# Cross-attention and mixture of experts on one core: scores computed transposed, DMA transposes replaced by block transposes and block moves

## The chip, the cores and the metric

The kernel runs on one core of a Trainium2 chip. The metric is device time in microseconds from start to end of one execution. TensorE (PE) multiplies matrices into PSUM, VectorE (DVE), ScalarE (ACT) and GpSimd (POOL) work on tiles of 128 partitions, and SyncE (SP) issues most DMAs.

## What is computed

One layer on x (4096 tokens, width 512) with a context of 3202 rows: cross-attention with a single head of width 512, then a top-2 router over 16 experts with a gated feed-forward of width 256 and a capacity of 512 rows per expert.

```python
x = x + attn(k=ctx, v=ctx, q=layernorm(x))        # softmax(q Wq^T (ctx Wk^T)^T / sqrt(512)) (ctx Wv^T + bv) Wo^T + bo
g = softmax(layernorm(x) @ w_router)              # 16 experts, the two highest are taken
h = silu(rows_e @ w_gate[e]) * (rows_e @ w_fc[e]) # rows_e: at most 512 rows of expert e
x = x + sum over the two experts of g * (h @ w_proj[e])
```

## The kernel before

Every f32 operand of a large product is split in two f16 parts, high and low, and `three_passes` (L41 to L47) multiplies high by high, high by low and low by high, so one product is three matmuls, on L45, L46 and L47. The program has three blocks that follow one another.

`setup` folds the weights (Wq with Wk into `m_w`, Wv with Wo into `g_w`), then turns the 25 full context tiles with a DMA transpose each (`transpose_c`, L194) into `cT`, and computes keys `kT` (512 wide, transposed) and values `vv` in eight PSUM banks. The context has 25 x 128 + 2 rows; the last two are "the tail". Their values are computed at the end of the block and written three times into `v_tail` by DMA (L299). The first query is prepared here as well.

`attend` goes through 32 tiles of 128 queries. TensorE's `step(t)` computes the scores of tile t + 1 (`scores`, 7 chunks: 6 of 512 keys and one of 130; the queries are the stationary operand and the keys stream) and then the values of tile t (`times_values`, 25 key tiles x 3 matmuls of 512 columns, then one matmul for the tail, L1036). VectorE copies each chunk out of PSUM and takes its maximum on the way (`evacuate`, L818), so that the maximum of a query is a number per partition. ScalarE takes the exponential of the whole row with that number as its bias and adds it up on the way (L760), then makes the high part (L765), and VectorE the low part (L840). Two DMA transposes of 25 blocks each (`transpose_p`, L653) turn these into `pT`, keys on partitions, as the product with the values needs them. Queries (`transpose_q`, L618) and router rows (`store_rows`, L635) are turned by DMA transposes too; only the last rows are turned by TensorE (`rows_T`). After the values `residual` on VectorE adds the residual and takes the statistics, GpSimd the power for the deviation, and `route` and `place` choose experts and positions. GpSimd scatters the choice to a table in DRAM. The order of work on each engine is the order in which the code is written; engines meet in semaphores alone.

`experts` gathers each expert's rows from DRAM, turns them on TensorE (L1502), multiplies (`up`, `down`), scales on ScalarE (`out_rows`) and scatters with addition on GpSimd (L1248); at the end the sums are loaded, corrected and stored.

## Time and profile before

| | us |
|---|---|
| median of 3 runs | 1644.28 |
| lowest, highest | 1640.95, 1647.89 |
| the profiled execution, its own time | 1646.86 |
| its span | 1645.0 |
| PE busy in the span | 1542.0 (94%) |
| DVE, ACT, POOL busy | 822.8, 444.7, 342.7 |

Times in the rows are microseconds from the span's start unless marked ns. A matmul's record lasts longer than its share of the engine, since matmuls are pipelined: what one costs in a stream is the distance between two starts. "Idle before" in brackets is time in which the engine had no work, and behind the arrow stands what released it.

### The profile page before, as it was taken

The page shows a single profiled execution, that of the slowest core. Times are in us where ns is not written, and L with a number is a line of the kernel's source. Part 1 is how long each engine was busy: PE and PEld are TensorE (multiplying, and loading weights), DVE is VectorE, ACT ScalarE, POOL GpSimd, SP SyncE. Part 2 cuts the span into 40 slices and gives each one's busy share as a digit, 9 for nine tenths or more (in the row PEclk, how much of TensorE's full clock was granted, in tenths as well). Part 3 has the DMA queues.
Part 4 walks back from the last instruction along what each step waited for, and adds up shares of the span by engine and source line. Part 5 has one row for each costly group of instructions (what it writes and reads, how often), then busy time and mean ns, then how long its engine had stood idle before and what let it go on. Part 6 is the DMA issues. An engine that isn't in the chain of part 4 may idle for free. (4 is left out here: it accounts for less than half of the span.)

```text
span 1645.0 us, 23544 instructions
## 1 busy us (share of the span) xinstructions
PE 1542.0 (94%) x7953; PEld 723.1 (44%) x7953; DVE 822.8 (50%) x2323; ACT 444.7 (27%) x537; POOL 342.7 (21%) x449
## 2 busy tenths in 40 slices
PE   7999889999999999999999999999996499999953
PEld 3444434444444444444444444444442245555520
DVE  4433245555555555554555555555554555555524
ACT  2332131231123212221222122311230244545430
POOL 1000001111111121112111211111111455665530
PEclk9999999999999999999999999999998699999975
DMA  7542135543554345434543454335432479899769
GB/s 211 119 102 49 52 73 118 105 91 78 110 112 91 78 103 120 91 78 96 120 97 78 88 121 96 86 80 118 102 83 62 141 187 232 200 205 223 153 105 370
DMA packets 372863, 198.52 MB, mean 121 GB/s; under 512 B 309528, under 2 KB 325918, under 8 KB 372832
## 3 DMA queue, kind: packets, MB, share of 16 engines
q1 hardware_dynamic: 350368, 154.04, 39.7%
q0 software_dynamic: 16896, 35.42, 11.4%
q10 hardware_dynamic: 5568, 8.67, 1.4%
q8 instruction: 17, 0.28, 0.1%
q14 instruction: 14, 0.11, 0.0%
HBM read 78.78 MB, written 43.81 MB: 75 GB/s over the span
## 5 line engine op out<-in xcount | busy, mean ns | idle before, releaser
L45 PE MATMUL sc<-kT,qt 128*128 128x512 f16 (+1 forms) x896 | 316.8, 359 | 9.4 <-PEq L184 4.9
L46 PE MATMUL sc<-kT,qt 128*128 128x512 f16 (+1 forms) x896 | 316.4, 358 | 0.0
L47 PE MATMUL sc<-kT,qt 128*128 128x512 f16 (+1 forms) x896 | 314.6, 358 | 0.0
L47 PE MATMUL acc<-vv,pT 128*128 128x512 f16 x775 | 293.6, 379 | 0.0
L46 PE MATMUL acc<-vv,pT 128*128 128x512 f16 x775 | 293.6, 379 | 0.0
L45 PE MATMUL acc<-vv,pT 128*128 128x512 f16 x775 | 293.5, 379 | 0.0
L818 DVE TENSOR_SCALAR_CACHE_REDUCE s_sb<-sc 128x512 f32<-128x512 f32 (+1 forms) x224 | 141.3, 631 | 194.6 <-PE sc L47 194.6
L771 ACT ACTIVATE row<-xs 128x512 f16<-128x512 f32 x32 | 20.2, 630 | 566.9 <-DVE xs L869 566.9
L840 DVE TENSOR_TENSOR p_hl<-p_sb,p_hl 128x3200 f16<-128x3200 f32 (+2 forms) x33 | 111.8, 3391 | 59.1 <-ACT p_hl L765 59.1
L45 PEld LDWEIGHTS sc<-kT,qt 128*128 128x128 f16 x896 | 88.0, 98 | 109.1 <-issue 19.1
L47 PEld LDWEIGHTS sc<-kT,qt 128*128 128x128 f16 x896 | 88.1, 98 | 92.0 <-issue 2.4
L46 PEld LDWEIGHTS sc<-kT,qt 128*128 128x128 f16 x896 | 88.1, 98 | 88.4 <-issue 2.0
L1248 POOL DMA_INDIRECT y_dram<-o_sb,sidx x64 | 102.4, 1601 | 103.0 <-ACT o_sb L1291 86.4
L760 ACT ACTIVATE p_sb<-s_sb,negb 128x3202 f32<-128x3202 f32 x32 | 95.0, 2970 | 87.7 <-DVE negb L826 87.7
L47 PEld LDWEIGHTS acc<-vv,pT 128*128 128x128 f16 x775 | 75.7, 98 | 91.6
L718 POOL TENSOR_TENSOR idf<-ia,ic 128x2 f32<-128x2 f32 x32 | 6.3, 197 | 520.8 <-DVE ia L926 520.8
L46 PEld LDWEIGHTS acc<-vv,pT 128*128 128x128 f16 x775 | 75.7, 98 | 80.7
L45 PEld LDWEIGHTS acc<-vv,pT 128*128 128x128 f16 x775 | 75.6, 98 | 80.8
L765 ACT ACTIVATE p_hl<-p_sb 128x3200 f16<-128x3200 f32 (+2 forms) x33 | 91.9, 2789 | 2.9
L858 DVE SCALAR_TENSOR_TENSOR x<-acc,rinv,xb 128x512 f32<-128x512 f32 x32 | 24.0, 751 | 130.4 <-PE acc L1036 130.4
L731 POOL TENSOR_TENSOR rstd_q<-var_q,nhalf 128x1 f32<-128x1 f32 x31 | 17.1, 550 | 281.3 <-DVE var_q L936 281.3
L1238 POOL DMA_INDIRECT rows<-rows_dram,gidx x64 | 67.8, 1059 | 34.1 <-issue 18.9
(247 smaller groups left out, 2154.5 us busy)
## 6 DMA issues: line engine op xcount, KB each, us to landing
xq<-in_x_dram SPq DMA_DIRECT2D x32, 256.0 KB, 2.8
x_in<-in_x_dram SPq DMA_DIRECT2D x32, 256.0 KB, 3.0
raw_g<-in_L_ffn_w_gate_dram SPq DMA_DIRECT2D x16, 512.0 KB
raw_f<-in_L_ffn_w_fc_dram SPq DMA_DIRECT2D x16, 512.0 KB
raw_p<-in_L_ffn_w_proj_dram SPq DMA_DIRECT2D x16, 512.0 KB
y_dram<-x SPq DMA_DIRECT2D x32, 256.0 KB, 3.0
rows_dram<-row SPq DMA_DIRECT2D x32, 256.0 KB, 2.2
y_sb<-y_dram SPq DMA_DIRECT2D x16, 512.0 KB, 17.4
```

Of the source, the lines that this page charges most:

```text
L45: pe.matmul(out, s_hi, m_hi, start=first, stop=False)
L46: pe.matmul(out, s_hi, m_lo, start=False, stop=False)
L47: return pe.matmul(out, s_lo, m_hi, start=False, stop=last)
L731: pool.tensor_tensor(rstd_q[:], var_q[:], nhalf[:], ALU.pow).then_inc(q_rstd, 1)
L760: act.activation(p_sb[:], s_sb[:], ACT.Exp, bias=negb[:], scale=SM / (XN_S * CTX_S), accum_out=rsum[:]).then_inc(exp_done, 1)
L765: act.activation(p_hl[:, 0, a * P:b * P], p_sb[:, a * P:b * P], ACT.Copy).then_inc(p_hi, 1)
L771: act.activation(row16[:, 0:D], xs2[:], ACT.Copy, scale=XN_S).then_inc(xs_hi, 1)
L818: dve.tensor_scalar(s_sb[:, 512 * c:512 * c + width[c]], sc[c % 3][:, 0:width[c]], 1.0, None, ALU.mult, ALU.max, accum_out=mxc[:, c:c + 1] ...
L840: dve.tensor_tensor(p_hl[:, 1, a * P:b * P], p_sb[:, a * P:b * P], p_hl[:, 0, a * P:b * P], ALU.subtract).then_inc(p_lo, 1)
L858: dve.scalar_tensor_tensor(out=x1[:], in0=acc[:], scalar=rinv[:], in1=xb[:], op0=ALU.mult, op1=ALU.add).then_inc(x1_rdy, 1)
L1238: pool.indirect_dma_start(rows[:, e % 2, 2 * D * j:2 * D * (j + 1)], None, rows_dram, bass.IndirectOffsetOnAxis(ap=gidx[:, e, j:j + 1], ax ...
L1248: pool.indirect_dma_start(y_dram, bass.IndirectOffsetOnAxis(ap=sidx[:, e, j:j + 1], axis=0), o_sb[:, e % 2, j, :], None, bounds_check=Y_LA ...
```

## The change

In `setup` the context tiles and the first two queries are turned by TensorE (`turns`) in two extra PSUM buffers and copied out by ScalarE and VectorE in turn; keys and values go through six banks in one sequence (`items`). The tail's values are computed as full tiles with the tail row repeated (`cT_wide`), so that no DMA is needed. In `attend` the keys are the stationary operand and the queries stream, so the scores come out transposed, keys on partitions, 128 columns per matmul. The maximum of a query then lies across partitions: it is folded on VectorE, turned by TensorE (`greatest`), reduced, made a diagonal and spread to all partitions by a matmul with ones (`spread`), and subtracted before the exponential. The sum is taken by GpSimd (`sums`) and a matmul with ones (`row_sum`). The scores buffer `s_T` exists twice. The tail has its own small scores and is added on VectorE in `residual`. Queries and router rows are turned in 32 x 32 blocks by VectorE, stored in DRAM, and loaded back block by block. In `experts` the end is in another order and its last products use four banks. The core of the diff:

```diff
 # setup, TensorE
+                def turns(kind, n):
+                    i = job[kind, n]
...
+                    for q in range(2 * KT):
+                        last = pe.transpose(turn[i % 2][:, q * P:(q + 1) * P], rows[:, q * P:(q + 1) * P], ident16[:])
+                    last.then_inc(t_pe, 1)
+                for i in range(TAIL):
...
+                    for t in range(KT):
+                        last = three_passes(pe, vt_bank[i][:],
+                                            (cT_wide[:, t * TAIL + i, :], cT_wide[:, (KT + t) * TAIL + i, :]),
+                                            (g_w[:, t, 0, :], g_w[:, t, 1, :]), t == 0, t == KT - 1)
+                        keys(n, k)
+                        if G4 * (n + 1) + k < NK:
+                            turns("c", G4 * (n + 1) + k)
 # attend, SyncE
+                def blocks_in(dest, blocks, done):
+                    for i in range(NB):
+                        sp.dma_start(dest[BL * i:BL * (i + 1)].rearrange("d k (g c) -> d k g c", c=BL),
+                                     blocks.rearrange("(g d) (k i c) -> i d k g c", d=BL, i=NB, c=BL)[i]).then_inc(done, 16)
-                    for h in range(2):
-                        sp.dma_start_transpose(pT[:, h], p_hl[:, h]).then_inc(pT_in, 16)
+                    if post:
+                        store_x1(t - 1)
+                        store_rows(t - 1)
+                        store_row_blocks(t - 1)
+                    if more_q:
+                        load_xq(t + 3)
+                    if post:
+                        load_row_blocks(t - 1)
+                    if turn_q:
+                        turn_query(t + 2)
 # attend, ScalarE
+                def copied(t, h, c):
+                    a, b = chunk[c]
+                    act.wait_ge(sc_pe, NCH * t + c + 1)
+                    if not isinstance(t, int) or t > 1:
+                        act.wait_ge(p_lo, NG * (t - 2) + group_of(a) + 1)
+                        act.wait_ge(sum_rdy, t - 1)
+                    act.activation(s_T[h][:, a:b, :].rearrange("p k c -> p (k c)"), sc[c % 3][:, 0:(b - a) * P],
+                                   ACT.Copy).then_inc(sc_cp, 1)
+                    if not isinstance(t, int) or t > 0:
+                        act.wait_ge(pv_part, NG * (t - 1) + g + 1)
+                    act.activation(pT[:, 0, a:b, :], s_T[h][:, a:b, :], ACT.Copy).then_inc(p_hi, 1)
 # attend, VectorE
+                        dve.tensor_tensor(rm[:, 0:b - a, :], so_far, s_T[h][:, a:b, :], ALU.max)
...
+                    dve.wait_ge(mx_pe, t + 1)
+                    dve.reduce_max(mx[:], ps_x[:, 0:P + TAIL], AX_X)
+                    dve.drain()
+                    dve.tensor_scalar(diag[:], ident[:], mx[:], None, ALU.mult).then_inc(dg_rdy, 1)
...
+                    dve.wait_ge(mb_pe, t + 1)
+                    dve.tensor_copy(m_b[:], ps_y[:, 0:P]).then_inc(mb_rdy, 1)
+                    dve.drain()
+                    for g, (a, b) in enumerate(groups):
+                        dve.tensor_tensor(s_T[h][:, a:b, :], s_T[h][:, a:b, :], m_b[:].unsqueeze(1).to_broadcast([P, b - a, P]),
+                                          ALU.subtract).then_inc(sub_rdy, 1)
+                    dve.transpose(row_bl[:], row16[:]).then_inc(rb_rdy, 1)
+                    dve.transpose(q_bl[:], q16[:]).then_inc(qb_rdy, 1)
 # attend, TensorE
+                    for n in range(a, b):
+                        for k in range(KT):
+                            keys_high, keys_low = (kT[:, h * KT + k, n * P:(n + 1) * P] for h in range(2))
+                            last = three_passes(pe, sc[c % 3][:, (n - a) * P:(n - a + 1) * P], (keys_high, keys_low),
+                                                (q_t[:, k, :], q_t[:, KT + k, :]), k == 0, k == KT - 1)
+                def greatest(t):
+                    pe.wait_ge(rm_rdy, t + 1)
+                    pe.transpose(ps_x[:, 0:P], rm1[:], ident[:]).then_inc(mx_pe, 1)
+                def spread(t):
+                    pe.wait_ge(dg_rdy, t + 1)
+                    wait_for(pe, rinv_rdy, t)
+                    pe.matmul(ps_y[:, 0:P], ones_f[:], diag[:], start=True, stop=True).then_inc(mb_pe, 1)
+                def row_sum(t):
+                    pe.wait_ge(sum_rdy, t + 1)
+                    pe.wait_ge(mb_rdy, t + 1)
+                    pe.matmul(ps_y[:, P:P + 1], sum1[:], ones_f[:, 0:1], start=True, stop=True).then_inc(rs_pe, 1)
+                        if k == 0:
+                            row_sum(t)
+                        if more and k == 3:
+                            greatest(t + 1)
+                        if more and k == 6:
+                            spread(t + 1)
+                        if post and k == (12 if more else 18):
                             logits(t - 1)
 # experts, TensorE
-                step(E // 2 - 1, 1, True, False)
                 for j in range(J):
-                    down(E - 1, j, 1)
+                    down(E - 2, j, 0)
+                for u in range(4):
+                    up(E // 2 - 1, 1, u)
+                last_down(E - 1, 1)
```

How this moves instructions is seen best on three queues. PE in the loop's body where scores end and values begin, now: the scores are followed by the tail's scores into ps_x, then values with the three f32 pieces in between.

```order
L47 MATMUL sc<-qt,kT 128x128
L45 MATMUL ps_x<-kT,qt 128x2
...
L47 MATMUL acc<-vv,pT 128x512
L1245 MATMUL ps_y<-ones_f,sum 128x1
...
L1234 MATMUL ps_x<-ident,rm 128x128
...
L1240 MATMUL ps_y<-diag,ones_f 128x128
```

Before, L47 of the last chunk (128x130) was followed by values at once, and one matmul (L1036) came at their end. The sum now stands after the first key tile, the transpose of the maxima after the fourth, the spread after the seventh.

VectorE in the loop's body from the fifth full chunk of scores to the fold of the maxima, now (rm is the running maximum, s_T the scores, rs_v and rinv belong to the tile before):

```order
L998 TENSOR_TENSOR rm<-rm,s_T 128x512
L1139 SCALAR_TENSOR_TENSOR q<-xqs,q 128x512
L996 REGISTER_ALU
L998 TENSOR_TENSOR rm<-rm,s_T 128x128
L1028 TENSOR_TENSOR rs_v<-p_tail 128x1
L1029 COPY p_held<-p_tail 128x2
L1032 TENSOR_TENSOR rs_v<-ps_y,rs_v 128x1
L1034 TENSOR_SCALAR rs_v<-rs_v 128x1
L1036 RECIPROCAL rinv<-rs_v 128x1
L1003 TENSOR_TENSOR rm<-rm 128x256
L1005 TENSOR_TENSOR rm<-rm 128x128
```

Before, the same place read:

```order
L818 TENSOR_SCALAR s_sb,mxc<-sc 128x512
L944 SCALAR_TENSOR_TENSOR q<-xqs,q 128x512
L815 REGISTER_ALU
L818 TENSOR_SCALAR s_sb,mxc<-sc 128x130
L824 TENSOR_REDUCE mx<-mxc 128x1
L826 TENSOR_SCALAR negb<-mx 128x1
```

The inverse of the sum has moved from the step's start to this place, and it waits there for TensorE's `row_sum`.

SyncE's loop body now:

```order
L735 DMA x_in<-in_x_dram 128x512
L739 ISA
L739 DMA y_dram<-x 128x512
L743 ISA
L743 DMA rows_dram<-row 128x1024
L753 DMA blocks_r<-row_bl 128x1024
L732 ISA
L732 DMA xq<-in_x_dram 128x512
L756 REGISTER_ALU
L748 DMA xrT<-blocks_r 32x32x32 x4
L762 DMA blocks_q<-q_bl 128x1024
```

and behind these four loads of qt from blocks_q (L748). Before, the body began with the two transposes of p_hl (L653) and had one transpose each for row and q.

## Rows read from the trace of the kernel before

**Rows 1.** Stretch: length; busy (count) PE, PEld, DVE, ACT, POOL; PEclk, DMA, GB/s.

```profile
228.90:1224.00 995.10, 995.10 (x5118) 461.43 (x5115) 523.90 (x1772) 228.88 (x236) 147.33 (x263) 1.00 0.45 97
```

**Rows 2.** Timeline of PE, one step: start us, us, engine line op, operands.

```profile
610.04 0.38 PE L47 MATMUL acc<-vv,pT 128*128 128x512 f16 x1
610.35 0.39 PE L1036 MATMUL acc<-v_tail,tailT 6*128 6x512 f16 x1
610.67 0.39 PE L45 MATMUL sc<-kT,qt 128*128 128x512 f16 x1
610.89 0.38 PE L46 MATMUL sc<-kT,qt 128*128 128x512 f16 x1
...
643.54 0.39 PE L1036 MATMUL acc<-v_tail,tailT 6*128 6x512 f16 x1
```

**Rows 3.** Timeline of PE in that step: the last chunk of scores, and the router's matmuls.

```profile
626.33 0.22 PE L45 MATMUL sc<-kT,qt 128*128 128x130 f16 x1
...
627.00 0.38 PE L45 MATMUL acc<-vv,pT 128*128 128x512 f16 x1
...
628.95 0.25 PE L1057 MATMUL ps_m<-w_r,xrT 128*128 128x32 f16 x4
...
629.15 0.38 PE L45 MATMUL acc<-vv,pT 128*128 128x512 f16 x1
```

**Rows 4.** Timeline of PE in setup: f32 matmuls of 128 columns.

```profile
43.34 1.05 PE L454 MATMUL bank<-ident,raw_g 128*128 128x128 f32 x8
```

**Rows 5.** Groups by form: line engine op operands xcount | busy us, mean ns | idle before.

```profile
L258 ACT ACTIVATE kT<-bank 128x512 f16<-128x512 f32 x24 | 14.3, 597 | 39.9 <-PE bank L47 39.9
L944 DVE SCALAR_TENSOR_TENSOR q<-xqs,q 128x512 f16<-128x512 f32 x31 | 21.3, 687 | 0.0
L313 DVE SCALAR_TENSOR_TENSOR kT<-bank,kT 128x130 f16<-128x130 f32 x4 | 1.2, 291 | 0.9 <-ACT kT L258 0.9
L1355 DVE COPY xTe<-tp 128x1024 f16<-128x1024 f16 x32 | 22.0, 688 | 13.8 <-PE tp L1502 8.6 <-issue 5.2
L1350 DVE SCALAR_TENSOR_TENSOR wp<-raw_p,wp 128x1024 f16<-128x1024 f32 x16 | 19.4, 1215 | 0.0
L840 DVE TENSOR_TENSOR p_hl<-p_sb,p_hl 128x3200 f16<-128x3200 f32 x31 | 108.3, 3493 | 59.1 <-ACT p_hl L765 59.1
L45 PEld LDWEIGHTS sc<-kT,qt 128*128 128x128 f16 x896 | 88.0, 98 | 109.1 <-issue 19.1
```

**Rows 6.** Timeline of DVE: small operations that wait for one another.

```profile
629.65 0.17 DVE L892 SCALAR_TENSOR_TENSOR lg<-ps_m,lg 128x16 f32<-128x16 f32 x1
629.90 0.17 DVE L878 TENSOR_REDUCE m<-lg 128x1 f32<-128x16 f32 x1
```

**Rows 7.** DMA: ScalarE's queue in 0 to 8 and 0 to 14 us; issues, us to landing.

```profile
q10 hardware_dynamic: 373, 0.26, 13.2%
...
q10 hardware_dynamic: 1204, 0.27, 11.6%
...
rows_dram<-row SPq DMA_DIRECT2D x32, 256.0 KB, 2.2
...
qt<-q SPq DMA_TRANSPOSE x32, 3.5
```

**Rows 8.** Timeline of PE: starts after idle time in setup and first tiles.

```profile
13.73 0.55 PE L432 MATMUL bank<-ident,tail_f 2*128 2x2 f32 x4 [2.07 <-DMA tail_f<-in_ctx_dram]
...
47.81 0.38 PE L45 MATMUL bank<-cT,m_w 128*128 128x512 f16 x1 [3.42 <-DMA cT<-c]
...
186.82 0.58 PE L45 MATMUL sc<-kT,qt 128*128 128x512 f16 x1 [4.85 <-PEq L184]
...
210.02 0.58 PE L45 MATMUL sc<-kT,qt 128*128 128x512 f16 x1 [4.55 <-DMA qt<-q]
```

**Rows 9.** Timeline of PE and POOL: last logits of attention, last expert's scatter.

```profile
1268.97 0.29 PE L1057 MATMUL ps_m<-w_r,xrT 128*128 128x32 f16 x4 [0.52 <-DVE xrT L992]
...
1584.91 1.54 POOL L1248 DMA_INDIRECT y_dram<-o_sb,sidx  x1 [5.41 <-DMA y_dram<-o_sb,sidx]
```

More of the change, by code:

```diff
@@ L300, in _ @@
-                act.wait_ge(s_vt, 48)
+                        item_high(n, "k", k)
+                        if late is not None:
+                            turned("c", late)
+                        late = G4 * (n + 1) + k if G4 * (n + 1) + k < NK else None
+                        if k == 2 and n in x_after:
+                            query_high(x_after[n])
+                    item_high(n, "v", 0)
+                    if late is not None:
+                        turned("c", late)
+                    for j in range(1, G4):
+                        item_high(n, "v", j)
+                        if j == 2 and n in x_after:
+                            turned("x", x_after[n])
@@ L377, in _ @@
                     dve.wait_ge(w_hi, KT + u + 1)
[L378 removed]
+                    dve.scalar_tensor_tensor(out=m_w[:, u, 1, :], in0=m_bank[u][:], scalar=W_S, in1=m_w[:, u, 0, :],
                                              op0=ALU.mult, op1=ALU.subtract).then_inc(w_lo, 1)
+                turned("c", 3)
                 for n in range(NC):
[L382 removed]
+                    late = None
+                    for k in range(G4):
@@ new lines, in _ @@
+                        if late is not None:
+                            turned("c", late)
+                        late = G4 * (n + 1) + k if G4 * (n + 1) + k < NK else None
+                        if n in x_after:
+                            query(x_after[n], k)
+                    item_low(n, "v", 0)
+                    if late is not None:
+                        turned("c", late)
+                    for j in range(1, G4):
+                        item_low(n, "v", j)
+                        if j == 2 and n in x_after:
+                            turned("x", x_after[n])
@@ L489, in attend, with group_of @@
     R12, PP, P12, OH2, tot1 = (v[n] for n in ("R12", "PP", "P12", "OH2", "tot1"))
-    NCH = -(-S // 512)
-    width = [min(512, S - 512 * c) for c in range(NCH)]
-    SKIP = float(1 << 20)
-    NK_A = (NK + 1) // 2
-    parts = ((0, NK_A), (NK_A, NK))
+    CH = 4
+    NCH = -(-NK // CH)
+    chunk = [(CH * c, min(CH * (c + 1), NK)) for c in range(NCH)]
+    groups = ((0, 2 * CH), (2 * CH, 4 * CH), (4 * CH, NK))
+    NG = len(groups)
+    SKIP = float(1 << 20)
+    BL = 32
+    NB = P // BL
+    assert TAIL == 2
+    def group_of(tile):
+        return [a <= tile < b for a, b in groups].index(True)
     with ExitStack() as c_:
@@ L779, in query_high, with step @@
                 def query_high(t):
-                    act.wait_ge(q_xs, t)
-                    act.wait_ge(q_in, 16 * t)
+                    act.wait_ge(q_xs, t - 1)
+                    wait_for(act, qb_rdy, t - 2)
                     act.activation(q16[:, 0:D], xqs[:], ACT.Copy, scale=XN_S).then_inc(q_hi, 1)
-                def step(t, post, more, more_q):
-                    if post:
+                def step(t, h, post, more, more_q, copies=True):
+                    for c in range(NCH if more and copies else 0):
+                        copied(t + 1, 1 - h, c)
+                        if c == 2 and post:
+                            rows_high(t - 1)
+                        if c == 4 and more_q:
+                            query_high(t + 2)
+                    if post and not more:
@@ new lines, in _ @@
+                exponentials(0, 0, 1)
+                copied(1, 1, 4)
+                high(0, 0, 1)
+                exponentials(0, 0, 2)
+                copied(1, 1, 5)
+                high(0, 0, 2)
+                copied(1, 1, 6)
+                query_high(2)
+                step(0, 0, False, True, True, False)
+                step(1, 1, True, True, True)
+                with act.Fori(1, NT // 2 - 1) as m:
+                    for h in range(2):
+                        step(2 * m + h, h, True, True, True)
@@ L1031, in times_values @@
                             logits(t - 1)
[L1032 removed]
+                        if post and k == (23 if more else NK - 1):
                             places(t - 1)
[L1035 to L1047 removed]
```

821 lines of the change are left out of this document (462 added, 359 removed).

## The prediction

> **What bounds the kernel now.** I read the stretches first, then TensorE's order of time inside one step, then the groups of the other engines and the DMA queues, and last the edges where TensorE is idle. From 228.90 to 1224.00 us TensorE is busy for all of 995.10 us at granted clock 1.00, the 2.4 GHz level, while VectorE is busy 524 us, ScalarE 229 and GpSimd 147 [rows 1]. Busy time alone could hide slow matmuls, so I checked the spacing. One step of the loop over query tiles runs from the tail matmul at 610.35 to the next at 643.54, 33.19 us; inside it a 512-column matmul follows the last after 0.215 us, and the tail lies in 0.63 us (610.04 to 610.67) [rows 2]. The twelve 130-column matmuls take 627.00 - 626.33 = 0.67 us, 56 ns each, and the eight of the router 0.20 us (628.95 to 629.15) [rows 3]. So 72 x 0.2155 + 0.67 = 16.19 us for scores, 75 x 0.2155 = 16.16 for values, 0.2 for the router, about 0.06 for places, 0.63 - 0.215 = 0.41 for the tail and 0.1 for its transpose make 33.1. Nothing in the step waits. The DMA transposes and all softmax work are hidden already: **the steady step gains nothing from what is removed**, and everything new on TensorE is paid 30 times.
>
> **The change, part by part.**
>
> *TensorE's step.* Scores become 25 x 4 x 3 = 300 matmuls of 128 columns. At 56 ns per 130 columns [rows 3] that is 55.5 ns each: 16.65, +0.46. The two tail keys become 12 matmuls of 2 columns, each with a full weight load; the router's narrow ones cost 0.20 / 8 = 25 ns, so +0.3. The old tail (0.41 + 0.1) goes. Three f32 pieces come in: the sum over keys, the transpose of the maxima, the spread of the maximum. Eight f32 records of 128 columns took 1.05 us [rows 4], at most 0.13 each; five records, two of them one column wide: +0.5. Together 33.19 + 0.46 + 0.3 - 0.5 + 0.5 = about 33.9, **+0.74 per step** (0.5 to 0.9).
>
> *A new wait on TensorE.* The transpose in `greatest` stands after four key tiles of values (the PE rows of the order), and behind it waits the rest of values, the whole engine. Let T be the start of values. The transpose is reached at T + 12 x 0.2155 + 0.2 = T + 2.8. Before that the fifth full chunk of scores ends at T - 0.84 (0.33 of tail and 0.67 of the last chunk lie behind it, less a drain); ScalarE copies it (0.60), VectorE takes the maximum (512 wide, 0.69), the low part of the query (0.69), the maximum of the last tile (0.29) [rows 5], the five small operations of `inverse`, 0.25 apart [rows 6], and folds of 256 and 128 elements (0.43 by the same rate, 0.29). This adds up to T + 3.3, and the f32 weight load after it is exposed, 0.2: a stall of 0.75 us. VectorE may also be behind at its head: between chunks 2.67 us apart it now does the block transpose of a row (1024 elements f16, between a copy of that size, 0.69, and a two-input operation, 1.22 [rows 5]) and the query's statistics. At 1.22 this makes ScalarE's `query_high` late, and the copy of the fifth chunk stands behind it: another 0.65. I take **1.0 us per step**, between the two (0 if VectorE overlaps more than I allow; 2 if each of the dozen handovers costs 0.1 more). The next new matmul, `spread`, comes 1.9 us later and needs about 1.3: free.
>
> *VectorE, ScalarE, GpSimd.* Per step VectorE does maxima 3.8, folds, diagonal and broadcast copy 1.6, subtraction of the maximum 3.8 and low parts 3.8 (3200 elements at 3.49 us, in three pieces [rows 5]), two block transposes 2.4, residual passes and statistics 3.3, and some 9 of query, rows, routing and places: about 28 of 34 us, against 17.5 now. ScalarE does about 13. GpSimd gets sums of 3456 elements; even at twice VectorE's time each that is 8 us, beside its 5. None becomes the bound by its sum; VectorE matters by its order alone. The first two thirds of the probabilities are ready some 18 us ahead of their use; the last third waits for values to end and is used 16 tiles into the next.
>
> *DMA.* Gone are two transposes of 25 blocks and two of 8. New per step are two stores of 256 KB (2.2 us, as rows_dram [rows 7]) and twice 4 loads of 1024 pieces of 64 bytes. SP waits in its queue for the query's and the row's blocks, with the next tile's loads behind; those have a whole step. For the pieces: in the first 8 us ScalarE's queue moved 373 packets in 13.2% of 16 x 8 us, in the first 14 us 1204 in 11.6% of 16 x 14 [rows 7]; the 831 between, nearly all of 4 bytes, cost (26.0 - 16.9) / 831 = 11 ns. On the other side the DMA transpose of a query, 1024 packets, lands after 3.5 us [rows 7]. So the four loads, 256 packets on each of 16 engines, take between 256 x 11 ns + 2 = 5 us and 4 x 3.5 = 14 us. I take 7, nearer the tiny packets, since these are plain packets too. Queries: blocks leave VectorE at T + 6.5, are in DRAM at 8.8 and turned at about 16; scores want them at T + 18. Rows: turned at about T + 7, wanted at T + 10. Hidden, with 2 to 3 us to spare.
>
> *Setup and the first tiles.* TensorE now turns 25 context tiles and 2 queries: 27 x 8 x 55.5 ns = +12.0. The two tail values are 24 matmuls instead of 12: +2.6. Against this, no wait for context transposes and no cold clock after it (3.42 idle [rows 8]), -5.4; projections no longer behind tail_f (2.07 [rows 8] and the ScalarE copies after), -2.7; no v_tail DMAs in the 4.85 before attention [rows 8], -3.4; second scores not after a DMA (4.55 idle, then cold again [rows 8]), -6. The two scores cost +1.6, more constants +1.5, and the first values wait for the first sums, +3. Together **+3**.
>
> *Last step and tail.* Rows of tile 30 go through DRAM while only values run: turned about 20 us after the step began, logits wanted at 12, and places and routing stand before the last residual: +6. Then the last row's blocks cost 1.2 + 2.3 + 7 instead of the 1.9 us that ended with the logits at 1268.97 [rows 9], plus two residual passes, 1.5: +10. Together **+16**.
>
> *Experts' end.* The last scatter waited 5.41 us for the previous expert's [rows 9], whose outputs now are written a whole `up` earlier: **-5**.
>
> Sum: 30 x 1.74 = 52, + 3 + 16 - 5 = **+66 us**. The profiled execution took 1646.86 us (span 1645.0), 0.2% over the median of 1644.28; I apply the sum to the median: **1710 us**.
>
> **The rivals.**
> 1. *Long narrow streams run slower than twelve do.* For: nothing here shows 300 in a row. Against: the spacing does not grow from the first to the twelfth, 56 ns [rows 3]. A weight load record lasts 98 ns [rows 5]; if loads no longer hid under matmuls half as long, a step would cost 300 x (98 - 55.5) = 12.8 us more, and even half of that is 1710 + 32 x 6.4 = 1915. It shows from 3 ns a matmul on. 4 in 100. The Trainium skill (TensorE: Matmul & The Clock Gate, Back-to-back issue gap) gives about 81 ns for a sustained pair of weight load and 128-column matmul, which by its figure would make a step 7.7 us longer, an estimate of 1955 us; the trace's 56 ns disagrees.
> 2. *The block moves are late.* The query's loads have no slack left at 9 us and decide from there: at 10, 1740; at 14 scores wait 5 us a step and the rows' loads hold logits 4 more, 1710 + 30 x 5 to 30 x 9 = 1860 to 1980. For: no 64-byte packets in the trace, and SP issues eight such loads a step. Against: 4-byte packets at 11 ns. 16 in 100, more than half of it at the small end. The Trainium skill (VectorE: DVE Perf Modes, The three transpose paths) warns that a plain DMA copy that transposes by strides is 19 times slower than a DMA transpose where the innermost destination stride is large. By its factor one query would take 66 us and the kernel over 3000; no run shows it, and the 64-byte runs here are whole.
> 3. *Not slower: the edges pay for the steps.* Its place is VectorE's chain between the last scores and `greatest`. If that ends before T + 2.8, and a 128-column matmul costs only its columns at 2.4 GHz, 53.3 ns, a step is 33.19 - 0.2 + 0.3 - 0.5 + 0.5 = 33.3; then 30 x 0.1 = +3, and with the first stretch at -4, the end of attention at +6 and the experts at -7 the sum is -2: 1642. It decides where the step stays under 33.4. Against: 56 ns is measured, and tail scores and f32 pieces are real work. 7 in 100, of which 3 pass to faster.
> 4. *The new wait never shows*, the rest as forecast: 1680. This is the low end of my case, not beside it.
>
> **The numbers.** My case, a step of 33.7 to 36 us: 73 in 100, 1710. Its bounds are +20 (30 x 0.5, and edges +5) and +109 (30 x 2.8, and edges +25), 1664 to 1753; the small end of rival 2 takes the top to 1775. Range **1664 to 1775**; it leaves out rival 1, rival 3 and the rest of rival 2, 18 in 100. A measurement of this kernel tells 0.5%, 8 us, from no change. Faster by more 0.03, within 0.04, slower 0.93.
>
> **What would show it.** In the profile after: a step of 34.3 to 35.5 us; narrow matmuls 55 to 56 ns apart; before `greatest` an idle TensorE of about 1 us, released by VectorE's fold; none before scores from the loads of qt, none before logits from those of xrT until the last step, which has 6 to 9; first values at about 228. It is wrong if the step is under 33.5 or over 36, or if the query's loads release the scores.

## The result, and the profile after

The changed kernel takes **1823.08 us** (median of 4 runs, 1821.14 to 1826.18) against 1644.54 for the kernel before on the same chip (1640.95 to 1647.89): ratio **1.109**, interval 1.106 to 1.112. Slower was forecast, but by 66 us; it is 178.5, and 1823 lies above the range. The profiled execution took 1826.18 us, its span 1824.5, that is 179.5 more than the span before. I cut both spans at the same four events, from TensorE's timelines:

| Stretch | before, us | after, us | more | forecast |
|---|---|---|---|---|
| start to the first values | 229.0 | 236.5 | +7.5 | +3 |
| 30 steps, first values to values of tile 30 | 995.5 (33.18 each) | 1156.3 (38.54 each) | +160.8 | +52 |
| from there to the experts' first table matmul | 61.3 | 77.3 | +16.0 | +16 |
| experts | 359.3 | 354.4 | -4.9 | -5 |

The start, the end of attention and the experts differ from the forecast by 4.6 us together, nearly all of it at the start; a step costs 5.36 us more where 1.74 was written. The stretches after, first the 30 steps, then a stretch of 38.74 us that ends at the transpose in `greatest`, about one step, and two pieces behind that transpose (length; busy time and count of PE, PEld, DVE, ACT, POOL; PEclk, DMA share, GB/s):

```profile
236.51:1392.79 1156.28, 1062.34 (x12051) 765.79 (x12052) 928.00 (x1864) 365.74 (x566) 514.39 (x503) 0.97 0.27 54
664.20:702.94 38.74, 34.34 (x403) 25.14 (x403) 32.08 (x66) 12.27 (x19) 17.26 (x17) 1.00 0.29 57
702.94:704.18 1.24, 1.24 (x6) 0.64 (x7) 0.80 (x4) 0.06 (x1) 0.00 (x0) 1.00 0.50 47
704.18:708.00 3.82, 3.82 (x12) 1.80 (x11) 2.47 (x3) 0.24 (x1) 0.00 (x0) 0.55 0.18 69
```

TensorE, busy all the time before [rows 1], is idle 94 us of these steps. VectorE went from 17.5 us a step to 928.00 / 30 = 30.9, and 32.1 in the stretch of 38.74. The last row is TensorE near the 1.2 GHz level. TensorE's timeline around `greatest` and the list of its waits show where both come from:

```profile
702.94 0.33 PE L1234 MATMUL ps_x<-ident,rm 128*128 128x128 f32 x1 [3.41 <-DVE rm L1005]
703.10 0.38 PE L45 MATMUL acc<-vv,pT 128*128 128x512 f16 x1
...
704.98 0.63 PE L46 MATMUL acc<-vv,pT 128*128 128x512 f16 x1
705.40 0.63 PE L47 MATMUL acc<-vv,pT 128*128 128x512 f16 x1
```
```profile
PE ps_x L1234 <- DVE rm L1005: 93.9, 30, 3.5
PE ps_m L1274 <- DMA xrT<-blocks_r: 17.7, 1, 17.7
```

The wait is the one forecast, at its place and with its releaser, VectorE's fold; but it lasts 93.9 / 30 = 3.1 us, not 1.0. From 704.2 on its matmuls are 0.43 us apart instead of 0.215. This does not happen in every step: slow matmuls stand behind 19 of the 30 transposes, 7 to 12 at a time, and cost 31 us in all, 1.0 us a step on average. From the fourth step on a step without them lasts 37.8 us (37.76 from the transpose at 665.18 to the one at 702.94), a step with them 38.8 to 40.1. The second row is the last tile's router rows; it is the only wait for blocks.

Everything else on TensorE is as it was written. The narrow matmuls and the twelve of the tail, from its timeline ahead of the values that start at 696.64:

```profile
696.28 0.22 PE L47 MATMUL sc<-qt,kT 128*128 128x128 f16 x1
696.33 0.17 PE L45 MATMUL ps_x<-kT,qt 128*128 128x2 f16 x1
...
696.61 0.16 PE L47 MATMUL ps_x<-kT,qt 128*128 128x2 f16 x1
696.64 0.38 PE L45 MATMUL acc<-vv,pT 128*128 128x512 f16 x1
```

So why is VectorE late? Its own timeline around that transpose, and GpSimd's at the same moments. The small operations are those of [rows 6]; `hit` marks the highest logit, `oh` is the chosen expert as a row of ones and zeros:

```profile
689.87 1.68 DVE L998 TENSOR_TENSOR rm<-rm,s_T 128x512 f32<-128x512 f32 x1 [0.54 <-ACT s_T L898]
...
711.79 0.17 DVE L1073 TENSOR_REDUCE m<-lg 128x1 f32<-128x16 f32 x1
712.04 1.30 DVE L1075 SCALAR_TENSOR_TENSOR hit<-lg,m,rev 128x16 f32<-128x16 f32 x1
713.41 0.17 DVE L1078 TENSOR_REDUCE r<-hit 128x1 f32<-128x16 f32 x1
713.66 1.08 DVE L1080 TENSOR_SCALAR oh<-rev,r 128x16 bf16<-128x16 f32 x1
```
```profile
689.74 1.25 POOL L827 TENSOR_TENSOR xb<-x_in,bo_row 128x512 f32<-128x512 f32 x1
...
712.04 2.67 POOL L858 TENSOR_TENSOR sum<-sum,s_T 128x512 f32<-128x512 f32 x2 [0.39 <-issue]
714.92 4.22 POOL L858 TENSOR_TENSOR sum<-sum,s_T 128x512 f32<-128x512 f32 x3 [0.20 <-issue]
```

An operation on 16 numbers takes 1.30 us, a reduction of the same 16 numbers 0.17, and the slow ones coincide with GpSimd's additions. Over the whole run, the groups by form, of after, then of before:

```profile
L998 DVE TENSOR_TENSOR rm<-rm,s_T 128x512 f32<-128x512 f32 x128 | 120.4, 941 | 68.3 <-ACT s_T L898 57.9 <-issue 9.5
L1080 DVE TENSOR_SCALAR oh<-rev,r 128x16 bf16<-128x16 f32 x64 | 68.5, 1071 | 5.0
L1075 DVE SCALAR_TENSOR_TENSOR hit<-lg,m,rev 128x16 f32<-128x16 f32 x64 | 45.3, 708 | 5.4
L1093 DVE SCALAR_TENSOR_TENSOR lg<-oh,lg 128x16 f32<-128x16 bf16 x32 | 35.1, 1098 | 2.4
```
```profile
L880 DVE SCALAR_TENSOR_TENSOR hit<-lg,m,rev 128x16 f32<-128x16 f32 x64 | 15.0, 235 | 5.4
L885 DVE TENSOR_SCALAR oh<-rev,r 128x16 bf16<-128x16 f32 x64 | 15.0, 234 | 5.3 <-issue 0.5
L898 DVE SCALAR_TENSOR_TENSOR lg<-oh,lg 128x16 f32<-128x16 bf16 x32 | 5.6, 175 | 2.4
```

That gave **theory A**: VectorE's queue sets the step, because GpSimd's new additions (L858, 860, 863) hold its operations up. **Rival B**: VectorE's total is beside the path; the badly placed wait at `greatest` and the slow clock behind it are the cost themselves.

### The profile page after: what moved, and what is told of

Read it like the earlier page. It is cut to its first block and busy times, and to the rows that moved or that the text cites. A ratio compares the mean times of both kernels' runs of the same rounds, so it can differ in the third digit from the quotient of the medians.

```text
span 1824.5 us, 40730 instructions
## 1 busy us (share of the span) xinstructions
PE 1620.5 (89%) x15565; PEld 1057.9 (58%) x15565; DVE 1253.2 (69%) x2427; ACT 602.0 (33%) x902; POOL 735.4 (40%) x708
## 5 line engine op out<-in xcount | busy, mean ns | idle before, releaser
L45 PE MATMUL sc<-qt,kT 128*128 128x128 f16 x3100 | 520.8, 219 | 3.4 <-POOL before L821 3.4
L46 PE MATMUL sc<-qt,kT 128*128 128x128 f16 x3100 | 520.9, 219 | 0.0
L47 PE MATMUL sc<-qt,kT 128*128 128x128 f16 x3100 | 520.8, 219 | 0.0
L47 PE MATMUL acc<-vv,pT 128*128 128x512 f16 x800 | 316.0, 395 | 0.0
L45 PEld LDWEIGHTS sc<-qt,kT 128*128 128x128 f16 x3100 | 303.3, 98 | 8.8 <-POOL before L821 3.9
L46 PEld LDWEIGHTS sc<-qt,kT 128*128 128x128 f16 x3100 | 303.3, 98 | 2.2
L47 PEld LDWEIGHTS sc<-qt,kT 128*128 128x128 f16 x3100 | 303.3, 98 | 0.0
L858 POOL TENSOR_TENSOR sum<-s_T 128x512 f32<-128x512 f32 x32 | 72.8, 2274 | 400.5 <-ACT s_T L909 400.5
L858 POOL TENSOR_TENSOR sum<-sum,s_T 128x512 f32<-128x512 f32 (+1 forms) x160 | 208.7, 1305 | 31.9 <-issue 17.4
L898 ACT ACTIVATE s_T<-sc 128x512 f32<-128x512 f32 (+1 forms) x224 | 118.2, 545 | 231.9 <-PE sc L47 216.9
L998 DVE TENSOR_TENSOR rm<-rm,s_T 128x512 f32<-128x512 f32 (+1 forms) x160 | 129.8, 811 | 73.2 <-ACT s_T L898 57.9
L909 ACT ACTIVATE s_T<-s_T,e_bias 128x1024 f32<-128x1024 f32 (+1 forms) x96 | 112.8, 1179 | 110.2 <-DVE s_T L1018 110.2
L47 PEld LDWEIGHTS acc<-vv,pT 128*128 128x128 f16 x800 | 80.7, 101 | 103.3 <-issue 15.3
L1024 DVE TENSOR_TENSOR pT<-s_T,pT 128x1024 f16<-128x1024 f32 (+1 forms) x96 | 127.7, 1354 | 6.1 <-ACT pT L918 6.1
L1018 DVE TENSOR_TENSOR s_T<-s_T,m_b 128x1024 f32<-128x1024 f32 (+1 forms) x96 | 116.2, 1266 | 2.9
L918 ACT ACTIVATE pT<-s_T 128x1024 f16<-128x1024 f32 (+1 forms) x96 | 104.3, 1087 | 27.5 <-PE acc L47 26.6
L1234 PE MATMUL ps_x<-ident,rm 128*128 128x128 f32 x32 | 11.9, 370 | 93.9 <-DVE rm L1005 93.9
```

What stands on the lines that cost most here:

```text
L45: pe.matmul(out, s_hi, m_hi, start=first, stop=False)
L46: pe.matmul(out, s_hi, m_lo, start=False, stop=False)
L47: return pe.matmul(out, s_lo, m_hi, start=False, stop=last)
L858: pool.tensor_tensor(sum4[:, 0:b - a, :], before_it, s_T[h][:, a:b, :], ALU.add)
L898: act.activation(s_T[h][:, a:b, :].rearrange("p k c -> p (k c)"), sc[c % 3][:, 0:(b - a) * P], ACT.Copy).then_inc(sc_cp, 1)
L909: act.activation(s_T[h][:, a:b, :], s_T[h][:, a:b, :], ACT.Exp, bias=e_bias[:], scale=SM / (XN_S * CTX_S)).then_inc(ex_rdy, 1)
```

## The experiments

Each ran against the kernel before on its own chip. Four chips were used, and the kernel before took 1644.1 to 1646.7 us on them, so runs of different groups can be compared to 2 or 3 us. "Step" is the start of values of tile 30 less that of tile 0, through 30; it comes from the profiled execution, the time is the median of all, and executions of one kernel differ by some 3 us, 0.1 us a step.

### e1_no_sums: GpSimd adds next to nothing

```diff
-                    for c in range(1, NCH):
...
-                        pool.tensor_tensor(sum4[:, 0:b - a, :], before_it, s_T[h][:, a:b, :], ALU.add)
...
+                    pool.wait_ge(ex_rdy, NG * t + NG)
                     wait_for(pool, rs_pe, t)
-                    pool.tensor_tensor(sum1[:], sum4[:, 0, :], sum4[:, 1, :], ALU.add).then_inc(sum_rdy, 1)
+                    pool.tensor_tensor(sum1[:], s_T[h][:, 0, :], s_T[h][:, 1, :], ALU.add).then_inc(sum_rdy, 1)
```

> Leaves out most of the sum over keys (one addition of two key tiles is left), so the row sum is not the real one; all else is as in the change. Theory A (VectorE's queue sets the step of 38.5 us, because GpSimd's additions hold up VectorE's small operations of route): the two operations on hit fall from 1.30 and 0.83 us to about 0.23 each, the two on oh from 1.08 to 0.24, the second on lg to 0.17, together 3.5 to 4.5 us less of VectorE's step; the wait before greatest falls from 3.1 us to under 1, step 34.3 to 35.5, time 1700 to 1735. Rival B (the wait at greatest comes from the order of the chain between the last scores and the transpose alone, what GpSimd does is beside the path): the wait stays at 3 us, step 38.4, time within 10 of 1823.

1723.37 us, ratio 1.048 (1.045 to 1.050); step 35.35. Its groups and its wait at `greatest`:

```profile
L991 DVE TENSOR_TENSOR rm<-rm,s_T 128x512 f32<-128x512 f32 x128 | 88.7, 693 | 103.7 <-ACT s_T L891 95.9 <-issue 7.0
L1068 DVE SCALAR_TENSOR_TENSOR hit<-lg,m,rev 128x16 f32<-128x16 f32 x64 | 16.0, 250 | 5.4
L1073 DVE TENSOR_SCALAR oh<-rev,r 128x16 bf16<-128x16 f32 x64 | 15.0, 234 | 4.9
```
```profile
PE ps_x L1227 <- DVE rm L998: 33.9, 30, 2.9
```

The operations are short again, and 100 us are gone. The wait is 33.9 / 30 = 1.1 us, about what the prediction had and a little over theory A's "under 1". Summed over its groups VectorE is busy 5.2 us less a step (oh 1.7, maxima 1.0, hit 0.9, lg 0.9, the rest low parts and placing); of this 3.2 comes off the step. B's "within 10 of 1823" is out.

The edit takes away the additions' length as well as the collisions, so GpSimd could also have been late by itself. The change's waits speak against it: inside the 30 steps VectorE waits for GpSimd nowhere. ScalarE waits nine times for a buffer that the additions still read, 14.5 us in all, and a step with such a wait (the one ending at 682.61) lasts 37.76 us, no longer than one without.

### e2_later and e3_later_twice: a better place for the wait, then more work on VectorE

```diff
-                        if more and k == 3:
+                        if more and k == 8:
                             greatest(t + 1)
-                        if more and k == 6:
+                        if more and k == 11:
                             spread(t + 1)
-                        if post and k == (12 if more else 18):
+                        if post and k == (14 if more else 18):
```

> The transpose of the maxima stands after 9 key tiles of values instead of 4, the spread after 12 instead of 7, the logits after 15 instead of 13. Theory A (VectorE's queue sets the step): TensorE no longer waits at greatest (under 0.5 us) and its clock stays at the 2.4 GHz level, but the idle time turns up elsewhere on TensorE; VectorE saves only what it waited for a slow TensorE, 0.5 to 1.5 us, step 37 to 38, time 1775 to 1808. Rival B (the wait of 3.1 us and the 1.6 us lost at the 1.2 GHz level behind it are the cost themselves): both go, step 33.9 to 34.2, time 1685 to 1695.

1817.16 us (1.105, 1.103 to 1.108), step 38.08: 0.46 less, though the medians differ by 5.9 us only. The wait at `greatest` is down to 4.0 us in all, and this row stands in its place:

```profile
PE ps_m L1284 <- DVE oh L1080: 98.4, 31, 3.2
```

The same 3 us are now spent in front of `places`, the matmuls that count the chosen experts. A's direction is right; its size was not reached (step 37 to 38 and 1775 to 1808 us expected), and the clock still falls, now behind 11 of these waits. B, with its 33.9 to 34.2, is refuted. The steps without slow matmuls last 37.8 us here too (389.89 to 427.66, from transpose to transpose), as in the change: moving the wait gained nothing on VectorE's chain, and what it gained is fewer slow matmuls.

e3 adds this to e2:

```diff
+                    dve.transpose(row_bl[:], row16[:])
+                    dve.drain()
                     dve.transpose(row_bl[:], row16[:]).then_inc(rb_rdy, 1)
```

> e2_later with the block transpose of the row made twice, 1.24 us more on VectorE per step. Theory A: the step grows by 1.0 to 1.3 us against e2_later, 30 to 39 us in all. Rival B (TensorE sets the step once the wait is gone, VectorE has slack): within 5 us of e2_later. If the growth is in between, VectorE sets only part of the step.

1849.00 us (1.125, 1.122 to 1.128), 31.8 over e2_later; the step grew by 1.03 us for 1.24 of work. VectorE has hardly any slack.

### e4_warm: the wait filled with matmuls

```diff
+        ps_z = c_.enter_context(nc.psum_tensor("ps_z", [P, 512], F32))
...
                         if more and k == 3:
+                            for _ in range(14):
+                                pe.matmul(ps_z[:], ident16[:], vv[:, 0, 0, :], start=True, stop=True)
                             greatest(t + 1)
```

> The change with 14 matmuls of 512 columns into an unused bank put before greatest, 3.0 us of work in the place of the 3.1 us of waiting; nothing else differs. It tells what the fall of the clock after the wait costs. If the slow matmuls are on the path (they delay the spread and the logits, for which VectorE waits 1.3 and 0.8 us): wait before greatest 0.1 to 1 us, clock 1.00 through the step, step 1.0 to 1.6 us shorter, time 1775 to 1795. If VectorE alone sets the step: step within 0.3 us of 38.5, time 1813 to 1833.

1809.04 us (1.100, 1.098 to 1.103), step 37.76, granted clock 1.00 in the 30 steps. Filling 3.0 us of waiting with useless work makes the kernel 14 us faster by the medians. In the profiles the step is 0.78 us shorter; of the 1.0 us that slow matmuls cost in a step on average, most is on the path, through VectorE's wait for `spread`, which falls from 36.0 us in all to 10.3. Every step is now as long as the change's steps without slow matmuls. The time lies between the two expectations.

### e5_no_sums_later: e1 and e2 together

> e1_no_sums and e2_later together: most of the sum over keys left out, and the transpose, the spread and the logits 5, 5 and 2 key tiles later. Theory A (GpSimd's additions slow VectorE, and with VectorE's queue shorter TensorE is the bound): the wait before greatest, 1.1 us a step in e1_no_sums, goes, and so does the slow clock behind it; the step is TensorE's own work, 33.9 to 34.2 us, time 1680 to 1695. Rival (VectorE's queue still sets the step without the contention): the wait moves to places or to logits, time within 8 of the 1723 of e1_no_sums.

1684.58 us (1.024, 1.022 to 1.026). In its 30 steps TensorE never stops:

```profile
230.86:1249.53 1018.67, 1018.67 (x12051) 758.80 (x12052) 795.81 (x1864) 363.56 (x566) 201.39 (x293) 1.00 0.30 62
```

The step is 33.96 us, TensorE's own work: **+0.78** over before, forecast +0.74. Later places were worth 0.46 us a step while VectorE was the bound (e2), 5.9 us by the medians; they are worth 1.39 now, 38.8 us by the medians. Of the 1.39, 1.13 is the idle time of e1. Another 0.22 lies around it: with the wait the matmuls before and behind the transpose start 1.69 us apart where 1.14 is idle, without it 0.32. The clock fell in e1 behind the first wait alone (2.94 us long, 0.05 us a step); behind the other 29, of 0.7 to 1.2 us, it stayed up. The same edit has at most a third of its value in front of a busy engine.

### e6_pe_sums_later: the sum over keys on TensorE

```diff
+                def row_sum(k):
+                    for h in range(2):
+                        last = pe.matmul(ps_z[:, 0:1], pT[:, h, k, :], ones16[:], start=(k == 0 and h == 0),
+                                         stop=(k == NK - 1 and h == 1))
...
+                        row_sum(k)
                         last = three_passes(pe, acc[:], (pT[:, 0, k, :], pT[:, 1, k, :]),
```

> The sum over keys is made by TensorE: 50 matmuls of one column a step, each key tile's high and low part times a column of ones, into a bank of its own; GpSimd adds nothing, the inverse is made ahead of the residual, and transpose, spread and logits stand later as in e2_later. Computes everything. Theory: step of e5_no_sums_later plus 50 times 25 ns (the router's matmuls), 35.1 to 35.4 us, time 1712 to 1735. Rival: a matmul of one column between wide ones exposes its weight load, 98 ns each: 3.6 us more a step, 1820 to 1840.

1715.99 us (1.044, 1.041 to 1.046), step 35.07. Two one-column matmuls and the next wide one, on its timeline:

```profile
700.31 0.38 PE L47 MATMUL acc<-vv,pT 128*128 128x512 f16 x1
700.52 0.19 PE L1231 MATMUL ps_z<-ones,pT 128*128 128x1 f16 x2
700.57 0.38 PE L45 MATMUL acc<-vv,pT 128*128 128x512 f16 x1
```

(35.07 - 33.96) / 50 = 22 ns each, with a full weight load each; the two in the rows take 700.57 - 700.52 = 0.05 us. TensorE never stops in these 30 steps. The kernel is 107 us faster than the change and 101 faster than e2_later, which has the same places: 10.7 us of GpSimd's additions a step are replaced by 1.1 us of TensorE.

### e7_memset: GpSimd writes but does not read

```diff
-                        pool.tensor_tensor(sum4[:, 0:b - a, :], before_it, s_T[h][:, a:b, :], ALU.add)
+                        pool.tensor_tensor(sum4[:, 0, 0:1], s_T[h][:, a, 0:1], s_T[h][:, a, 1:2], ALU.add)
+                        for _ in range(3):
+                            pool.drain()
+                            pool.memset(sum4[:, 0:b - a, :], 1.0)
...
```

> The change with GpSimd's additions over keys replaced by fills of the same buffer (three of the same size for each addition), so the row sum is not the real one; GpSimd is about as busy but hardly reads. If VectorE's operations are slow because both engines read on-chip memory at the same time: the operations on hit and lg, which take two inputs, fall to 0.2 us, time 1720 to 1745. If any work of GpSimd holds VectorE up: they stay at 0.8 to 1.3 us, time within 20 of 1823. The Trainium skill (SBUF: State Buffer, SBUF: two separate sides) states that the two engines share one pair of ports under an exclusive lock, that a VectorE operation with two inputs contends only with a GpSimd operation that reads, and that one in a fast mode contends with any: by it hit and lg become fast and oh, a one-input operation, may stay slow.

1896.74 us (1.153, 1.150 to 1.156), which neither side expected. The rows, though, answer the question:

```profile
L1082 DVE TENSOR_SCALAR oh<-rev,r 128x16 bf16<-128x16 f32 x64 | 20.6, 322 | 5.0
L1077 DVE SCALAR_TENSOR_TENSOR hit<-lg,m,rev 128x16 f32<-128x16 f32 x64 | 15.1, 235 | 5.4
L1095 DVE SCALAR_TENSOR_TENSOR lg<-oh,lg 128x16 f32<-128x16 bf16 x32 | 5.6, 176 | 2.4
L1060 DVE TENSOR_SCALAR xs<-x,mvb,rstdb 128x512 f32<-128x512 f32 x32 | 45.8, 1432 | 88.5 <-POOL rstdb L831 88.5
```

With fills beside them the two-input operations are as fast as alone; `oh`, with one tensor as input, is a little slow (322 against 234). The time went elsewhere: three fills of 0.53 us with their drains and the small addition ahead of them last longer than one addition, GpSimd reaches the deviation of the row late, and VectorE waits 88.5 us for it (last row). I had sized the replacement wrongly; as a timing it tells nothing of the theories.

### e9_psum_route and e10_psum_route_later: the routing's tensors out of the way

```diff
+        ps_r = c_.enter_context(nc.psum_tensor("ps_r", [P, 512], F32))
+        rev_p, lg_p, lg2_p = (ps_r[:, E * i:E * (i + 1)] for i in range(3))
...
-                    return dve.tensor_scalar(oh[:, k, :], rev[:], r12[:, k:k + 1], None, ALU.is_equal)
+                    return dve.tensor_scalar(oh[:, k, :], rev_p, r12[:, k:k + 1], None, ALU.is_equal)
...
-                    dve.scalar_tensor_tensor(out=lg2[:], in0=oh[:, 0, :], scalar=-1e30, in1=lg[:],
+                    dve.scalar_tensor_tensor(out=lg2_p, in0=oh[:, 0, :], scalar=-1e30, in1=lg_p,
```

> The change with three small tensors of the routing (the descending numbers, the logits, the logits without the greatest) in an unused bank of TensorE's accumulator memory, so that none of the five slow operations reads two inputs from the ordinary on-chip memory; GpSimd's additions stay. Computes everything. Theory (those operations wait because they and GpSimd's additions use the same way into that memory): on hit 0.70 us on average to 0.25, on oh 1.07 to 0.25, on lg 1.10 to 0.2, 3.5 us less of VectorE a step; time 1725 to 1750, of which 1723 (e1_no_sums) is the floor. Rival (GpSimd slows whatever VectorE does meanwhile): they stay slow, time within 10 of 1823. The Trainium skill (SBUF: State Buffer, SBUF: two separate sides) lets only operations in a fast mode or with two SBUF inputs contend, which is the theory's side.

> e9_psum_route with the transpose, the spread and the logits later, as in e2_later. Computes everything. Theory: with the contention mostly gone VectorE has slack again and TensorE's own 33.96 us a step is the bound, as in e5_no_sums_later at 1685: time 1690 to 1715. Rival: what contention is left (maxima beside the bias addition, low parts) keeps VectorE the bound, and the later places gain as little as in e2_later: 1720 to 1745.

e9: 1789.15 us (1.086, 1.083 to 1.089), step 37.39. e10: 1762.82 us (1.071, 1.068 to 1.073), step 36.37. They lie 39 and 48 us above what the theory expected of them, and neither rival fits. Groups of e10:

```profile
L1077 DVE SCALAR_TENSOR_TENSOR hit<-ps_r,m,rev 128x16 f32<-128x16 f32 x64 | 15.0, 234 | 5.5
L1082 DVE TENSOR_SCALAR oh<-ps_r,r 128x16 bf16<-128x16 f32 x64 | 15.0, 234 | 5.0
L1026 DVE TENSOR_TENSOR pT<-s_T,pT 128x1024 f16<-128x1024 f32 x64 | 108.3, 1732 | 1.7 <-ACT pT L920 1.7
L1113 DVE SCALAR_TENSOR_TENSOR ia<-r,off 128x2 f32<-128x2 f32 x32 | 36.6, 1142 | 0.0
L1107 DVE TENSOR_TENSOR P<-e_two,P 128x1 f32 x28 | 25.3, 902 | 4.7 <-issue 4.7
```

The mechanism held to the nanosecond for the moved operations (234 ns, as alone). But the additions go on for 10 us, and the next operations with two inputs, which stand where the moved ones ended, pay now: low parts 1732 instead of 1353 ns, `ia` 1142 instead of 394, `P` 902 instead of 352. Contention moved like the wait in e2.

### e11_few_turns: the block transposes cut short

```diff
-                    dve.transpose(row_bl[:], row16[:]).then_inc(rb_rdy, 1)
+                    dve.transpose(row_bl[:, 0:32], row16[:, 0:32]).then_inc(rb_rdy, 1)
```

(and the same for `q_bl`; two copies ahead of the loop fill both buffers once.)

> The change with VectorE's two block transposes cut to 32 of 1024 columns, so that queries and router rows after the first tiles are not the real ones; stores and loads of the blocks stay. Theory (VectorE's queue sets the step): 2 x 1.15 us less of it a step, step 36.2 to 36.6, time 1755 to 1770. Rival (the transposes lie in VectorE's waits for TensorE and ScalarE): under 0.5 us a step, 1810 to 1825.

1791.45 us (1.089, 1.086 to 1.092), step 37.50: 1.04 us less, between both. The query's transpose stands in front of VectorE's wait for `spread`; that wait grew from 36.0 us in all to 63.9. So 2.3 us of VectorE work cost about 1: VectorE sets the step together with the waits in its chain, not by its work alone.

### e12_before_adds: the additions in the kernel before

```diff
                         deviation_q(t + 2)
+                    for _ in range(8):
+                        pool.drain()
+                        pool.tensor_tensor(junk[:], junk[:], bo_row[:], ALU.add)
                     scatter(t - 1)
```

> The kernel before, computing everything, with eight additions of 128x512 f32 without any use put on GpSimd in each step, after the query's deviation, so that they run beside VectorE's routing; nothing of the change is in it. Theory (the contention is between GpSimd's additions and VectorE's operations, wherever they meet): on hit, oh and lg the same rows as in the change, 0.7 to 1.3 us instead of 0.23; in the kernel before VectorE has 4 us of idle time in the step and places comes 3.2 us after oh, so the time grows by 0 to 20 us only. Rival (the slow rows come of something else in the change, the place of its buffers or the two block transposes): the rows stay at 0.23 and the time within 5 us of 1644.

1667.62 us (1.013, 1.011 to 1.016), 23 more, a little over the 0 to 20 expected. Groups, and TensorE's timeline:

```profile
L885 DVE SCALAR_TENSOR_TENSOR hit<-lg,m,rev 128x16 f32<-128x16 f32 x64 | 68.4, 1069 | 5.4
L890 DVE TENSOR_SCALAR oh<-rev,r 128x16 bf16<-128x16 f32 x64 | 40.8, 637 | 5.3 <-issue 0.5
L903 DVE SCALAR_TENSOR_TENSOR lg<-oh,lg 128x16 f32<-128x16 bf16 x32 | 38.8, 1213 | 2.4
```
```profile
680.04 0.19 PE L1072 MATMUL ps_m<-oh,before 128*128 128x32 bf16 x1 [0.59 <-DVE oh L890]
```

The same rows without any of the change. The delay of nearly 4 us used up the 3.2 us between `oh` and `places`, and what was over became a wait of TensorE. On average `hit` and `lg` are slower than in the change and `oh` is less so (637 ns, just under the 0.7 expected).

### e8_before_experts: only the experts' end

The function `experts` of the change in the kernel before, nothing else.

> The kernel before with nothing of the change but the experts' end (the last expert's outputs held until all its gate and up products are made, four banks). The part of the span from the first table matmul to the end was 359.3 us before and 354.4 in the change. Theory: that 4.9 us is the experts' order alone, so time 1639 to 1641, ratio 0.997. Rival: it came from what attention leaves behind in the change, and the order alone gives under 1 us.

1639.73 us (12 runs, against 17), ratio 0.9972, interval 0.9961 to 0.9984: the 4.9 us belong to the experts' order. Of all kernels here **this one alone beats the kernel before**.

## Where the prediction was right and wrong

**The step that failed** is the sentence that costs GpSimd: "GpSimd gets sums of 3456 elements; even at twice VectorE's time each that is 8 us, beside its 5. None becomes the bound by its sum". The additions were priced as GpSimd's time and at nothing for anyone else. They last 10.7 us a step, and VectorE is 5.2 us busier for them (e1), so that with 30.9 us of work and half a dozen handovers it sets the step. This costs 38.54 - 35.35 = 3.19 us a step, 96 us in all, and no rival had it. Of it, 2.4 is VectorE's longer chain (37.76 - 35.35) and 0.8 the slow matmuls behind the longer waits (e4). The count of 3456 is off as well: a step adds 5 x 512 + 128 + 256 + 128 = 3072 elements.

The additions also make the first values 5.3 us later than in e1_no_sums. The timelines of both split this: about 2.7 us are maxima that run beside additions (before the query's statistics at 228.73), and 2.8 are GpSimd's own delay, since the deviation of the query stands behind the additions in its queue (VectorE waits 3.71 us for it, 0.92 in e1_no_sums).

Term by term, in us:

| Term | forecast | measured |
|---|---|---|
| TensorE's own step | +0.74 | +0.78 (e5) |
| wait at `greatest`, with the clock behind it | 1.0 | 1.39 (e1 less e5): 1.13 idle, 0.22 around it, 0.05 clock |
| GpSimd beside VectorE | 0 | 3.19 (after less e1), 0.78 of it by the clock |
| setup and first tiles | +3 | +2.2 without the additions (e1), +7.5 with |
| last step and tail | +16 | +16.0 |
| experts' end | -5 | -4.9 |

*TensorE's work* was right to 0.04 us, from twelve narrow matmuls and a few f32 ones. Rival 1 is out: 300 in a row are 55.8 ns apart (247.51 to 264.20 in e5_no_sums_later), so the Trainium skill's 81 ns for such a pair (TensorE: Matmul & The Clock Gate, Back-to-back issue gap) does not hold here.

*The wait* was right in place, releaser and mechanism. Its idle time of 1.13 us without contention is near the 1.0 of the forecast, part of it by luck: the terms given for its chain add up to T + 3.4, not T + 3.3, and the 0.22 around it was left out. That the clock can fall behind it was left out too; at 1.1 us it did not (e1), at 3.1 us it did in 19 of 30 steps.

*VectorE's total* of 28 us was too high for the work alone: 25.8 in e1_no_sums. What it lacked was the neighbour.

*The first stretch* had two forecasts, +3, which is 232 us for the first values, and "first values at about 228"; the scores were indeed done at 228.5, and the first low part came 7.8 us behind them.

*Block moves* were hidden in every step, as forecast, and rival 2 did not come. The issues of the change in a step (KB each, us to landing):

```profile
blocks_r<-row_bl SPq DMA_DIRECT2D x1, 256.0 KB, 2.0
xrT<-blocks_r SPq DMA_DIRECT2D x4, 64.0 KB, 3.4
blocks_q<-q_bl SPq DMA_DIRECT2D x1, 256.0 KB, 2.0
qt<-blocks_q SPq DMA_DIRECT2D x4, 64.0 KB, 3.0
```

In the tail (the last tile), where nothing hides them, four loads took 5.2 us from the first issue (1448.34) to the logits (1453.52), at the low end of "between 5 and 14", below the 7 taken. The factor of 19 quoted in rival 2 shows nowhere.

*The end of attention* came out at +16.0, but 6.7 of it have another cause. From TensorE's timeline:

```profile
1417.31 0.61 PE L45 MATMUL acc<-vv,pT 128*128 128x512 f16 x1 [7.37 <-DVE x L1047]
...
1453.52 0.29 PE L1274 MATMUL ps_m<-w_r,xrT 128*128 128x32 f16 x4 [17.67 <-DMA xrT<-blocks_r]
```

The +6 was written for rows that go through DRAM; no wait for them shows in the last step. In their place the last values wait 7.37 us for VectorE's residual, 0.64 before. The wait is 6.07 us in e5_no_sums_later and 5.0 in e1_no_sums, so most of it is not contention: behind the values come a high part, a low part and three passes, and no scores cover them any more. That the +16 was met is in part luck. The second row is the tail's, expected at about +10.

*Rivals 3 and 4* are answered by e5_no_sums_later: even with no wait and no contention the kernel is 2.4% slower, because the step is 33.96 and not under 33.4.

## What to carry to other kernels

Work put on an idle engine is free only if it does not slow the one that has none to spare: before moving streaming arithmetic to GpSimd, look at which of VectorE's operations will run beside it, and price each that reads two tensors from on-chip memory (here the one-input `oh` too) at up to the length of one of GpSimd's. A wait in front of an engine that is the bound cannot be removed by moving it (e2, 6 us for a wait of 94); shorten that engine's queue first, and the same move pays 39 us (e5). A term that comes out right in total can hide a wrong cause; the wait's releaser in the trace tells.

## What the runs showed of the hardware

- **GpSimd and VectorE get in each other's way.** Beside additions of 128x512 f32 (1.3 us each) a VectorE operation on 16 numbers takes up to 1.3 us instead of 0.23; reductions and operations that read the accumulator banks keep their 0.17 to 0.25 (after, e9, e12). GpSimd pays as well: the first addition of each step, beside VectorE's subtraction, takes 2.27 us on average instead of 1.3. Fills, which do not read, leave two-input operations alone (e7). The Trainium skill has the rule (SBUF — State Buffer, SBUF: two separate sides): the two share one pair of ports, locked for a whole instruction, and two inputs from SBUF (the on-chip memory) on VectorE contend only with a GpSimd operation that reads. The runs agree for the two-input operations: the `hit` of 712.04 starts and ends with an addition, 1.30 and 1.33 us, and beside fills it takes 0.235. `oh` has one tensor as input and is held up all the same, by additions (1.07) and a little by fills (0.32), so two inputs are not the only case. The rule was there to be read before the forecast and would have changed its largest term.
- **TensorE after a wait.** After 3.4 us of idle time before 702.94 the clock fell a little later, with a granted clock of 0.55 from 704.18 to 708.00, though TensorE was busy again by then; behind the next wait (2.95 us, before 741.74) the matmuls were slow from the first on, and behind the one after it (3.41 us, before 781.19) none was. Behind the 29 waits of 0.7 to 1.2 us in e1 none was. Fourteen useless matmuls in the wait kept the clock at 1.00 and shortened the kernel by 14 us (e4).
- **One-column matmuls** with a full weight load cost 22 ns each between wide ones, in pairs, 1500 times over (the steps of e6 and e5 compared); a row sum over keys is cheap there.
